# GpSimd's two-frequency product held back until VectorE's first even add, in a Fourier-attention and mixture-of-experts kernel

## What is computed

```python
s = sigmoid(norm(query, axis=-1))
for _ in range(10):
    s = 3.9 * s * (1.0 - s)
q = query * (1.0 + 0.1 * (s[..., None] - 0.5)) * (1.0 + 0.1 * wave[None, :, None])
Q, K, V = q @ Wq.T + bq, mem @ Wk.T + bk, mem @ Wv.T + bv
Qf, Kf, Vf = fft(Q, axis=-2), fft(K, axis=-2), fft(V, axis=-2)
QKV = hamilton(hamilton(Qf * filt, Kf * filt), Vf * filt)
x = x + ifft(QKV, axis=-2).real          # query = LN(x), memory = ctx
...
x = x + LN(x) + w * gelu(LN(LN(x)) @ wi[e]) @ wo[e]   # e, w: top-1 expert and its probability
```

## Time and profile before

| | us |
|---|---|
| median of 3 runs (3410.73 to 3417.0) | 3416.19 |
| the profiled execution, device time | 3416.19 |
| its span in the trace | 3414.4 |
| PE busy over the span | 3264.1 (96%) |
| DVE busy over the span | 2868.4 (84%) |
| ACT busy over the span | 2241.4 (66%) |
| POOL busy over the span | 1416.3 (41%) |

### The profile page before, as it was taken

One profiled execution on the slowest core, in us unless ns is written; L12 is line 12 of the kernel. 1 busy time (PEld: TensorE's weight loads), 2 busy tenths in 40 slices (PEclk: granted clock), 3 DMA queues, 4 the chain that ended last, 5 costly groups with the idle time before them and its releaser, 6 DMA issues. The chain is left out here.

```text
span 3414.4 us, 56375 instructions
## 1 busy us (share of the span) xinstructions
PE 3264.1 (96%) x17944; PEld 2687.3 (79%) x17944; DVE 2868.4 (84%) x3953; ACT 2241.4 (66%) x4838; POOL 1416.3 (41%) x1608
## 2 busy tenths in 40 slices
PE   7999999999999999999999669999999999999998
PEld 5777777777777777777777359998989898989997
DVE  4999999999999999999999757776767776767774
ACT  5666666676666666676666367776767676767764
POOL 3476767677676767676775500000000000000001
PEclk9999999999999999999999779999999999999999
DMA  6422221222121222212120233344434433333331
GB/s 227 148 100 75 88 74 62 74 75 86 62 86 62 87 74 75 92 59 83 62 100 26 75 107 111 109 123 124 125 113 124 125 124 101 112 113 111 123 98 42
DMA packets 299962, 327.61 MB, mean 96 GB/s; under 512 B 47600, under 2 KB 179056, under 8 KB 299760
## 3 DMA queue, kind: packets, MB, share of 16 engines
q1 hardware_dynamic: 284400, 308.12, 28.5%
q0 software_dynamic: 15360, 16.99, 1.4%
HBM read 256.96 MB, written 101.97 MB: 105 GB/s over the span
## 5 line engine op out<-in xcount | busy, mean ns | idle before, releaser
L1369 POOL TENSOR_TENSOR tally<-tally,unit 1x1 f32<-1x1 f32 x16 | 8.4, 523 | 1314.6 <-DVE res L1814 1314.6
L1471 PE MATMUL out_ps<-wo_h,act_h 128*128 128x512 f32 x1024 | 405.1, 396 | 0.0
L1472 PE MATMUL out_ps<-wo_h,act_l 128*128 128x512 f32 x1024 | 404.5, 395 | 0.0
L1473 PE MATMUL out_ps<-wo_l,act_h 128*128 128x512 f32 x1024 | 399.6, 390 | 0.0
L1803 DVE TENSOR_TENSOR act_l<-act,act_h 128x512 fp32r<-128x512 f32 x256 | 176.5, 690 | 257.3 <-ACT act_h L1638 257.2
L1773 DVE TENSOR_TENSOR wi_l<-w_sum,wi_h 128x1024 fp32r<-128x1024 f32 x128 | 156.9, 1226 | 116.5 <-ACT wi_h L1570 115.4
L1412 PE MATMUL y_bank<-tok_h,wi_h 128*128 128x256 f32 x768 | 222.2, 289 | 13.9 <-DVE tok_l L1739 6.3
L972 POOL DMA_INDIRECT slots<-rows,slot_i x128 | 212.3, 1659 | 46.5 <-issue 46.2
L1473 PEld LDWEIGHTS out_ps<-wo_l,act_h 128*128 128x128 f32 x1024 | 193.4, 189 | 43.4
L511 PE MATMUL pair<-w_qh,q_high 128*128 128x512 f32 x512 | 222.2, 434 | 1.5 <-ACT q_low L743 1.5
L1471 PEld LDWEIGHTS out_ps<-wo_h,act_h 128*128 128x128 f32 x1024 | 195.1, 191 | 29.4
(11 more groups left out here) (241 smaller groups left out, 11237.1 us busy)
## 6 DMA issues: line engine op xcount, KB each, us to landing
w_raw<-in_L_ffn_wi SPq DMA_DIRECT2D x256, 256.0 KB, 3.0
w_raw<-in_L_ffn_wo SPq DMA_DIRECT2D x128, 512.0 KB, 4.8
w_raw<-in_x SPq DMA_DIRECT2D x32, 1024.0 KB, 5.2
w_raw<-in_ctx SPq DMA_DIRECT2D x32, 1024.0 KB, 5.2
x_res<-in_x SPq DMA_DIRECT2D x31, 1024.0 KB, 5.3
out<-x_res SPq DMA_DIRECT2D x31, 1024.0 KB, 4.4
slots<-rows SPq DMA_DIRECT2D x4, 4160.0 KB, 16.6
got<-slots SPq DMA_DIRECT2D x15, 1040.0 KB, 7.6
```

What stands on the lines that cost most here:

```text
L1369: nc.gpsimd.tensor_tensor(tally[:], tally[:], unit[:], ALU.add).then_inc(tallied, 1)
L1471: nc.tensor.matmul(out_ps[t][:], ah, oh, start=(j == 0 and h == 0), stop=False)
L1472: nc.tensor.matmul(out_ps[t][:], al, oh, start=False, stop=False)
L1473: last = nc.tensor.matmul(out_ps[t][:], ah, ol, start=False, stop=(j == STEPS - 1 and h == 1))
```

## The change

One wait is added in `real_bins`, ahead of the two that were there: GpSimd waits until `unfold` has counted `(b - 1) * UNF + 1`. For sequence 0 the value is negative and no wait is emitted.

```diff
@@ -932,6 +932,7 @@
                             pool.wait_ge(consts_in, 16 * SETUP_DMAS)
                             ts(bias16[:], bias16[:], float(SEQ), 0.0, ALU.mult, ALU.add).then_inc(zeroed, 1)
                             pool.wait_ge(zeroed, ZEROED)
+                        wait(pool, unfold, (b - 1) * UNF + 1)
                         pool.wait_ge(real_loaded, b * 16 + 16)
                         wait(pool, real_stored, b * 16)
                         c = rc
```

## The result

The changed kernel took 3378.7 us (median of 4 runs, 3374.7 to 3379.2) against 3415.7 (4 runs, 3410.7 to 3417.0): a ratio of 0.9892 with a 95% interval of 0.9875 to 0.9909. That is 36.9 us less where 24 were forecast, and 1.3 us under the low end of the range. A second set of runs gave 0.9895 (0.9878 to 0.9911).

What follows compares the result with a forecast made beforehand. VectorE was taken as the bound, TensorE about 1.05 us behind. Per period 1.6 - 0.5 - 0.3 = 0.8 us, thirty times 24 us, so 3416.2 - 24 = 3392 us; range 3380 to 3411.

Steps and rivals of the forecast that it cites:

- low end of the range: Cheapest case, 3380 us: TensorE's busy 57.87 us floors a period, leaving 1.05 or 1.2 us a period to gain.
- gain at the old place: VectorE's instructions beside the chain (query folds, products, placing, sums) return to free durations: 1.61 us a period.
- wait for the third real row: VectorE waits for ScalarE's third real row, late behind `mean2`: 0.1 to 0.2 us a period.
- stretch of PSUM readers: The 3.04 us from L1156's end to L1010, where the chain's first instructions run without stalling VectorE.
- the rival that took the rule whole: Dear meetings: GpSimd fully blocks VectorE in four context folds, 1.2 us instead of 0.5; 3403 us, chance 0.14.
- term of 0.5 for what VectorE loses at the new place: Context folds: one small GpSimd instruction at each of four fold starts, 0.11 to 0.14 each; bounds 0.35 and 0.82.
- step on `q_of`: Late `scales1` operations meet products, so `q_of` ends at 1132 and VectorE's query fold waits 0.1 to 0.3 us.
- slower rival: GpSimd's lateness becomes the bound, paid at `q_of` after another lost meeting: 3428 or 3458 us, chance 0.12.
- Thirty times 0.8: Net gain of 0.8 us a period, counted for the 30 sequences 2 to 31: 24 us.

Runs made afterwards that it cites:

- wait3 run: The changed kernel with the added wait's count raised from + 1 to + 3, so the chain starts 1.3 us later: 3389.0 us, ratio 0.9916.
- split version: The changed kernel with the chain cut in two: first eight instructions, `mean1`, then the other seven: 3371.1 us; on one chip 3369.6 against 3377.5.
- cut kernels: The kernel before and the changed kernel, each with the chain's 15 instructions cut to one value on each of 16 partitions: 3368.8 and 3370.1 us.

## Why the prediction was off

**Held.** The bound (VectorE) and the mechanism: every forecast step of the gain at the old place came within 0.05 us of its size, and 0.09 that had no step came on top, 1.75 for 1.61 in all. The wait as such costs nothing. `mean1` has no idle time, the chain is 8.7 us long, the wait for the third real row is 0.31 in a short period and 0.18 in a long one, where 0.1 to 0.2 were forecast. The stretch of PSUM readers was free, as the Trainium skill has it (SBUF — State Buffer, "Who interferes with whom"). Of the same section's other rule, that the whole instruction blocks, the runs show for GpSimd that it waits up to the whole of a product (5.58 and 5.65 us for four multiplies), and for VectorE a loss of 0.12 by a 16 x 64 and none to be seen by a 16 x 1, so that the rival that took the rule whole did not come about.

**The step that failed: the term of 0.5 for what VectorE loses at the new place.** It is the term of the sum that was most mis-sized: 0.26 was measured. It counted one meeting at the start of each of four folds at 0.11 to 0.14. Two happened at that price. At L1011 there was none, since the first seven instructions end ahead of it and the eighth has to wait for its end. At L1016 one happened for nothing: the multiply got in around 1130.9, and L1016 took 0.69. There VectorE has a gap of its own: L1012 is issued 0.08 us before L1011 ends, while L1016, which needs L1012's result, starts 0.03 behind its end. The 0.14 that I had read as the price of a small instruction, L1015's in the earlier trace rows, was that of a 16 x 128 at the same gap, by the wait3 run. So the loss is 0.26, and 0.24 x 28 = 7 us more were gained.

**The step on `q_of`.** It had the five operations of `scales1` get in at one product's end each. In a short period of the changed kernel the first three ran in 0.20 us each ahead of the first product, two took 2.15 and 2.12, and `q_of` ended 2.0 us before VectorE wanted it. In a long one only the first was so quick. The other four took 2.30, 2.12, 1.06 and 1.06, and VectorE waited 0.36 for `q_of`, a little over the 0.1 to 0.3 of the forecast. Both waits together came to 0.31 and 0.54 by turns, and to nothing in six periods: 0.42 on average over the 22 others, 9 us in all, where 0.3 x 28 = 8 were forecast. So the step held about as forecast, and little of the miss lies here. The slack at `q_of` is used up in every second period, so the slower rival was near, as the prediction had it.

**"Thirty times 0.8."** Sequence 2 was counted at the price of a middle period. It gave 2.0 us, since its chain ran beside a fuller stretch than those in the loop, and sequence 1, counted as nothing since it did not move by much, gave 0.5: a start 0.48 us later takes the multiply by signs out of the folds. Before, its L1015 and L1016 took 0.96 and 0.94, now 0.69 and 0.80. VectorE's timeline of sequence 1, before and then after:

```profile
148.21 0.96 DVE L1015 TENSOR_TENSOR c_fold<-w_raw 128x512 f32<-128x512 f32 x1
149.09 0.94 DVE L1016 TENSOR_TENSOR c_fold<-w_raw 128x512 f32<-128x512 f32 x1
```

```profile
147.72 0.69 DVE L1016 TENSOR_TENSOR c_fold<-w_raw 128x512 f32<-128x512 f32 x1
148.34 0.80 DVE L1017 TENSOR_TENSOR c_fold<-w_raw 128x512 f32<-128x512 f32 x1
```

Together: 0.14 more gain and 0.24 less loss are 0.38 us a period, or 11 us in 28. The waits cost 1 more than forecast. Sequences 1 and 2 gave 2.5 where 0.8 was forecast, 1.7 more, and sequence 31, counted at 0.8, gave nothing. The pipeline's last two periods came out at -0.3. That is 24 + 11 - 1 + 1.7 - 1.1 = 34.6, against 34.8 measured between the odd adds. The medians differ by 36.9; the other 2 us lie in the scatter between executions. That the time fell out of the stated range, by 1.3 us, is chance: the four runs of the changed kernel spread over 4.5 us. That it fell near the range's low end and not near 3392 is not chance, but the terms above.

One reading of the earlier trace rows was loose without effect: GpSimd's 41.49 of 58.92 us are 70%, not two thirds or less.

**The low end of the range: TensorE's busy 57.87 as the floor of a period.** By this step at most 1.05 or 1.2 us a period were to be had, 36 us in all. It failed too, though the changed kernel's average of 57.84 in the loop hides it. Its short periods take 57.7, the six without waits gained 1.50 each, and the split version's loop takes 57.54 on average: its stage is 44.6 us shorter than before. TensorE's busy time in one period read 57.87, 57.56, 57.33, 57.22 and 57.07 for the same work, so one such reading is no floor.

**Open.** What sets the floor near 57.55: VectorE's wait of up to 0.5 us for ScalarE's real row in the cut kernels suggests a path from TensorE by ScalarE to VectorE, but no run shortened it. In the split version VectorE has no wait and is busy for 56.65 of 57.53, with as much between its instructions (0.88) as in the kernel before (0.85), so there it is as full as it was. Nor was a version that leaves the chain out altogether tried.

## What to carry to other kernels

Where the instructions of a side engine slow those of the engine that bounds, price each meeting by the size of the side instruction and by whether it falls into a gap of the other engine. Place the large ones (here 16 x 192, 0.4 us) in a stretch whose instructions read PSUM. If the chain is too long for such a stretch, cut it so that what others wait for, here the mean, stands between its parts. Count the first and last rounds of a pipeline by their own timelines, compare two periods in a row before one is taken for all, and don't take one reading of a busy time for a floor.

## What the runs showed of the hardware

- The price of a meeting to VectorE goes with the GpSimd instruction: 0 for 16 x 1, 0.12 for 16 x 64, 0.38 for 16 x 192. At the gap of 0.03 ahead of a fold that needs the result before it (L1015 of before), it was 0 for 16 x 64 and 0.13 for 16 x 128. That is no rule for every gap: L1118 in the earlier trace rows, behind a gap of 0.12, lost 0.11 beside a 16 x 64. To GpSimd it is up to the whole of the other's instruction, at any size: beside long products a multiply took 2.36 us with 16 x 64 and 2.24 with 16 x 1, and 0.31 and 0.18 in the free.
- VectorE's instructions on 128 x 4 numbers pay as much as long ones, and so most for their size: 0.35 on 0.17 us beside a 16 x 192, and 0.26 on 0.16 beside a 16 x 128.
- Small delays are rounded: a mean 1.0 us later cost VectorE no more wait (0.30 in a short period of both). The first of the statistics behind it took 1.41 us where it had taken 1.96, ending beside a product of VectorE in both, and so half of the delay was gone behind it.
